# A decoder block on one core: where the later feed-forward's weights are loaded beside the expert slots

## The chip, the cores and the metric

One core of one Trainium2 chip runs the whole program. The metric is the device time of one execution in microseconds. The kernel before was run three times: 704.51 us is the median, with 700.71 and 704.6 as the others.

## The reference, cut to what matters

The input is 16 sequences of 128 tokens with 256 channels, in fp32. Six residual blocks follow each other. Each normalizes x and adds its result to x:

```
x = x + attention_0(layernorm(x))           # 16 heads
x = x + long convolution with the context, gated by layernorm(x)
x = x + mixture of experts(layernorm(x))    # a shared expert, and 1 of 8 experts for each token
x = x + attention_1(layernorm(x))
x = x + attention over the context tokens (masked)
x = x + feed-forward(layernorm(x))          # 256 -> 1024 -> 256, with ternary weights
```

Two of them matter here. In the mixture of experts, each token takes the expert with the largest router logit, and adds `gate * expert(x)` and `shared(x)`. Both are `silu(x @ wg) * (x @ wu) @ wd`. The last block's two weight matrices (256 x 1024 and 1024 x 256) are made ternary: the mean of the absolute weights sets a scale, the weights are scaled, rounded and clipped to -1, 0, 1. That preparation depends on no activation, so it can be done at any earlier point.

## The kernel before, in words

x stays in SBUF as 16 tiles of 128 tokens. Each engine has its own stream, in which the stages follow each other, and semaphores are the only order between engines. The change lies in `experts` (lines 954 to 1429), in its calls into `feed_forward` (`sync_weights`, `act_weights`, `pe_weights`, `dve_weights`, lines 1605 to 1663), and in `memory_attention`'s `mask` (line 1459).

The stage of the experts runs so:

- **Routing.** The 16 tiles are normalized and the router's logits made. The shared expert's gate and up projections (L1109, `pe_half`) run beside it and after it. Each token gets a row in a sorted array: expert by expert, padded to 23 slots of 128 rows.
- **Scatter.** POOL issues 16 indirect DMAs (L1292), which write the normalized rows to `sorted_x` in HBM. After all of them, SP loads the slots' rows (`load_slot`, L1192) into two buffers in turn. Slot t waits until slot t-2 has been transposed.
- **Shared downs.** The shared expert's down projection (`pe_shared`, L1162; four matmul instructions for each tile) is added to x by DVE (L1170 before the slots, L1394 behind them). `DOWN_FIRST` tiles, 8 here, are done ahead of the slots and the rest behind them. PE and DVE alternate over two PSUM banks, so PE's tile n waits for DVE's tile n-2.
- **Slots.** 23 slots with two steps in flight. PE transposes the rows (L1204), does gate and up (L1229, expert number from a register), transposes h (L1221) and does the down (L1239). ACT copies and does silu, DVE multiplies (L1265) and copies y (L1270), and POOL stores y to `sorted_y` (L1275).
- **Return.** When the last y is stored, POOL gathers the rows back tile by tile (L1304), DVE adds them with the gate (L1403), and the second attention begins.

Work for later stages is placed beside the slots, by `beside_slots`, once a step after the slot steps 2 to 5. Step index 0 and 1: ACT's sums of absolute values of the two weights (L1623), and on DVE two constants and the two passes over the mask (L1462, L1464). Index 2: PE's sum over partitions (L1636), which also waits until DVE has copied the fourth y, and DVE's chain of four small operations (L1650 to L1653). Index 3: the rounding of the first matrix on ACT (L1628) and DVE (L1658, L1663). The second matrix is rounded behind the slots ("later", "later end"), between the remaining downs of DVE.

The order on SP around it is: the first matrix in one DMA of 1 MB when half of the scatters are done, then (all scatters done) slots 0, 1 and 2, half of the second matrix, slot 3, the other half, the mask, and then slots 4 to 22. Behind that, when both matrices are rounded, SP loads 1.5 MB of bias and norm rows (L1603), and with `w_done` this waits for DVE's last pass L1663.

`slots` writes the first 6 steps out, runs the middle ones in a loop of two steps and writes the last ones out. PE has no loop there.

Of the kernel before, what the change touches and what calls it, by code (L numbers as in the profile page):

```python
# [9 lines left out]
NB = 16  # L10
# [9 lines left out]
NS = (NB * P - NE) // P + NE  # L20
# [18 lines left out]
def wait(eng, sem, value):  # L39

    if isinstance(value, int) and value <= 0:
        return
    eng.wait_ge(sem, value)
# [48 lines left out]
def build(nc, a, out, stages=6):  # L92

    ctx = ExitStack()
    with ctx:
# [3 lines left out]
        def sem(name):  # L99
            return ctx.enter_context(nc.semaphore(name))  # L100
# [69 lines left out]
        moe_y = sem("moe_y")  # L170
        w_o_loaded = sem("w_o_loaded")
        rows_loaded, route_loaded = sem("rows_loaded"), sem("route_loaded")
# [781 lines left out]
        def experts(conv_done, beside_slots):  # L954
# [15 lines left out]
            f = Front(0, NB, lambda eng, t: eng.wait_ge(s["x_conv"], t + 1), own_x=True)  # L970
# [128 lines left out]

            DOWN_FIRST = 8
            def pe_half(pe, n, p, kt):
                c, k = p // 2, p % 2
                if kt == 0:
                    pe.wait_ge([s["sh_silu"], s["sh_h"]][k], 2 * n + c + 1)
                    if p == 0:
                        pe.wait_ge(f.xnT, f.base_T + 4 * n + 4)
                mm = pe.matmul(ps[4 + p], w_sh_gu[:, kt, k * D + c * P:k * D + (c + 1) * P],  # L1109
                               xnT_all3[:, kt, ds(n * 512, 512)],  # L1110
                               start=(kt == 0), stop=(kt == KT - 1), skip_group_check=True)
                if kt == KT - 1:
                    mm.then_inc(s[f"sh_{'gu'[k]}{c}"], 1)
# [57 lines left out]
                                          ALU.add).then_inc(s["x_shared"], 1)  # L1171


            def slots(name, eng, body, ahead, behind):

                first, last = 6, (NS - ahead) - (NS - ahead) % 2
                for t in range(first):
                    body(eng, t, t % 2, t // 2)
                    if t >= 2:
                        beside_slots(name, eng, t - 2)  # L1180
                with eng.Fori(first // 2, last // 2) as i:
                    for u in range(2):
                        body(eng, 2 * i + u, u, i)
                for t in range(last, NS + behind):
                    body(eng, t, t % 2, t // 2)
                    beside_slots(name, eng, t)
# [3 lines left out]
            def load_slot(sp, t, u):  # L1190
                wait(sp, s["xsT_ps"], t - 1)
                sp.dma_start(xs[u], sorted_x[ds(t * P, P), :]).then_inc(s[f"xs{u}"], 16)  # L1192
# [116 lines left out]
            def sync(sp):  # L1309
                sp.wait_ge(conv_done, 2 + 2 * CH)  # L1310
                load_context(sp)
                sp.wait_ge(gathered[5], 16 * (NB // 2))
                beside_slots("sp", sp, "weights 0")
                sp.wait_ge(s["scattered"], 16 * (NB // 2))
                for t in range(3):
                    load_slot(sp, t, t % 2)
                beside_slots("sp", sp, "weights 1")
                load_slot(sp, 3, 1)
                beside_slots("sp", sp, "weights 2")
                sp.wait_ge(s["x_shared"], 2 + DOWN_FIRST)  # L1320
                beside_slots("sp", sp, "mask")
                with sp.Fori(2, 2 + NB // 2) as i:
                    for u in range(2):
                        load_slot(sp, 2 * i + u, u)
                for t in range(4 + NB, NS):
                    load_slot(sp, t, t % 2)

            def tensor(pe):
                pe.wait_ge(conv_done, 2 + 2 * CH - 2)
                keep_busy(pe, ps[3], ident, 9)  # L1330
                pe.wait_ge(conv_done, 2 + 2 * CH)
                pe.wait_ge(route_loaded, 48)
                pe.wait_ge(moe_loaded, 32)
                for t in range(NB + 3):
                    pe_route(pe, t, t % 2, t // 2)
                    if t < 5:
                        keep_busy(pe, ps[7], ident, 2)
                    if t >= 6:
                        q, kt = divmod(t - 6, 2)
                        pe_half(pe, q // 4, q % 4, kt)  # L1340
                pe_half(pe, 1, 2, 1)
                pe_positions(pe)
                pieces(pe, pe_piece)
                pe_shared(pe, 0, DOWN_FIRST)
                pe.wait_ge(s["expert"], 1)
                pe.wait_ge(moe_loaded, 64)
                experts = {0: load_expert(pe, 0)}
                pe.wait_ge(s["sh_h"], 10)
                pe.wait_ge(s["x_shared"], 2 + DOWN_FIRST)
                keep_busy(pe, ps[5], ident, 6)  # L1350
                pe_turn_slot(pe, 0, 0, 0)
                for t in range(NS + 1):
                    pe_slot(pe, t, t % 2, t // 2, experts)
                    if 2 <= t < 6:
                        beside_slots("pe", pe, t - 2)
                pe.wait_ge(s["silu"], NS)
                pe_shared(pe, DOWN_FIRST, NB)

# [12 lines left out]
            def vector(dve):  # L1371

                dve.wait_ge(route_loaded, 48)
                dve.tensor_copy(tri_bf, tri).then_inc(bf_ready, 1)
                dve.memset(ones_bf, 1.0).then_inc(bf_ready, 1)
                dve.memset(tick, 0.0).then_inc(s["sh_h"], 2)
                dve.engine_nop().then_inc(s["x_shared"], 2)
                routing(dve, dve_route, dve_piece)
                dve_positions(dve)
                pieces(dve, dve_piece)  # L1380
                dve_gate(dve)
                dve_shared(dve, 0, DOWN_FIRST)
                slots("dve", dve, dve_slot, 0, 1)
                for t in range(DOWN_FIRST, NB - 2):
                    dve_down(dve, t)
                    if t == 9:
                        beside_slots("dve", dve, "later")
                    if t == 11:
                        beside_slots("dve", dve, "later end")
                dve_gathered(dve, 0, 1)  # L1390

# [170 lines left out]
        def feed_forward(x_ready, before):  # L1562
# [4 lines left out]
            f = Front(0, 3 * NB, x_ready)  # L1567
# [9 lines left out]
            w32_3 = [kt_x(w32[0], INNER), kt_x(w32[1], D)]  # L1577
# [27 lines left out]
            def sync_weights(sp, part):  # L1605


                cp = lambda ap: ap.rearrange("(c p) n -> p c n", p=P)
                if part == "weights 0":
                    sp.dma_start(w32_3[0], cp(a["ffn_w1"])).then_inc(route_loaded, 16)  # L1610
                else:
                    k = INNER // P // 2
                    part = slice(0, k) if part == "weights 1" else slice(k, 2 * k)
                    sp.dma_start(w32_3[1][:, part, :], cp(a["ffn_w2"])[:, part, :]).then_inc(s["w_loaded"], 16)

            def act_weights(act, t):
                if t in (0, 1):
                    if t == 0:
                        act.wait_ge(route_loaded, 48 + 16)
                    else:  # L1620
                        act.wait_ge(s["w_loaded"], 32)
                    wait(act, s["w_abs"], t)
                    act.activation(junk_w, w32[t], ACT.Abs, accum_out=wabs[:, t:t + 1]  # L1623
                                   ).then_inc(s["w_abs"], 1)
                if t in (3, "later"):
                    act.wait_ge(s["w_chain"], 2)
                    k = 0 if t == 3 else 1
                    act.activation(w32[k], w32[k], ACT.Identity, bias=c_magic,  # L1628
                                   scale=wscale[:, k:k + 1]).then_inc(s["w_scaled"], 1)

            def pe_weights(pe, t):
                if t == 2:
                    pe.wait_ge(s["ones"], 1)
                    pe.wait_ge(s["w_abs"], 2)
                    pe.wait_ge(moe_y, 4)
                    pe.matmul(ps[7][:, D:D + 2], ones, wabs, start=True, stop=True).then_inc(s["w_tot"], 1)  # L1636

            def dve_weights(dve, t):
# [462 lines left out]
        def for_later_stages(name, eng, t):  # L2101

            if name == "sp":
                if t == "mask":
                    memory.sync(eng)
                else:
                    ffn.sync_weights(eng, t)
            if name in ("act", "pe", "dve"):
                ffn.weights[("act", "pe", "dve").index(name)](eng, t)
            if name == "dve":  # L2110
                memory.mask(eng, t)

        moe = experts(conv.summed, for_later_stages)

# [12 lines left out]
        memory = memory_attention(attn1.x_ready)  # L2127
# [105 lines left out]
```

## Time and profile before

| | |
|---|---|
| median of 3 runs | 704.51 us (700.71, 704.51, 704.6) |
| span of the profiled execution | 711.1 us |
| PE / DVE / ACT / POOL busy | 617.1 / 518.5 / 399.1 / 335.0 us |
| from the scatter's first issue to the first slot's transpose | 274.2 to 306.4 us |
| the slots, from the first transpose to the last y | 306.4 to 385.2 us |
| the rounded weights' last pass on DVE | 388.6 to 389.8 us |
| first work of the second attention on PE | 394.9 us |

The page gives no time of the profiled execution beside its span. That span is 6.6 us longer than the median of the runs and 10.4 us longer than the fastest of them. "Idle before" in brackets is the time for which an engine had nothing to run, with the instruction or transfer that ended it. A PE row's duration includes the modelled end of its last matmul.

### The profile page before, as it was taken

The page shows a single profiled execution, that of the slowest core. Times are in us where ns is not written, and L with a number is a line of the kernel's source. Part 1 is how long each engine was busy: PE and PEld are TensorE (multiplying, and loading weights), DVE is VectorE, ACT ScalarE, POOL GpSimd, SP SyncE. Part 2 cuts the span into 40 slices and gives each one's busy share as a digit, 9 for nine tenths or more (in the row PEclk, how much of TensorE's full clock was granted, in tenths as well). Part 3 has the DMA queues.
Part 4 walks back from the last instruction along what each step waited for, and adds up shares of the span by engine and source line. Part 5 has one row for each costly group of instructions (what it writes and reads, how often), then busy time and mean ns, then how long its engine had stood idle before and what let it go on. Part 6 is the DMA issues. An engine that isn't in the chain of part 4 may idle for free.

```text
span 711.1 us, 15833 instructions
## 1 busy us (share of the span) xinstructions
PE 617.1 (87%) x4620; PEld 471.5 (66%) x4622; DVE 518.5 (73%) x1187; ACT 399.1 (56%) x826; POOL 335.0 (47%) x650
## 2 busy tenths in 40 slices
PE   6999999989998899689999689999999677557776
PEld 5788888875555764477887567888887433245554
DVE  3688999985999674125224569999999578688994
ACT  2577777773333133034332246777777467778992
POOL 1234655444997344411112445333332568475882
PEclk9899999999999799799999779999999899859999
DMA  8301400011348701432221310000000000000101
GB/s 290 129 3 36 168 0 0 0 32 29 67 67 347 260 0 53 141 127 75 78 86 43 142 38 24 2 3 0 0 0 1 1 1 1 0 0 1 35 25 60
DMA packets 23043, 42.07 MB, mean 59 GB/s; under 512 B 3056, under 2 KB 18048, under 8 KB 21840
## 3 DMA queue, kind: packets, MB, share of 16 engines
q1 hardware_dynamic: 19504, 31.14, 13.9%
q0 software_dynamic: 3488, 10.28, 4.3%
q8 instruction: 29, 0.48, 0.3%
q14 instruction: 22, 0.18, 0.1%
HBM read 31.15 MB, written 10.26 MB: 58 GB/s over the span
## 4 chain that ended last, share of the span: by engine, by line
PE 55%; issue 14%; DVE 14%; POOL 8%; ACT 7%; DVEq 1%; DMA 1%; another core or an unknown queue 0%; SPq 0%; POOLq 0%; ACTq 0%
PE ps L1229 6%; PE ps L335 5%; PE ps L363 5%; PE ps L373 4%; PE ps L1109 4%; PE ps L383 3%; PE ps L322 3%; POOL ctx_sb L891 3%; PE ps L345 3%; DVE work L577 3%; PE ps L1239 3%; PE ps L802 2%; PE ps L1162 2%; DVE work L583 2%; PE ps L1883 2%
## 5 line engine op out<-in xcount | busy, mean ns | idle before, releaser
L498 ACT COPY wide<-ps 128x512 f32<-128x512 f32 x126 | 74.5, 593 | 43.3 <-PE ps L335 41.3
L230 POOL TENSOR_TENSOR var_eps<-mv,powers 128x1 f32<-128x1 f32 x80 | 16.8, 210 | 160.6 <-DVE mv L221 160.5
L577 DVE TENSOR_REDUCE work<-ps 128x8 f32<-128x1024 f32 x64 | 77.9, 1217 | 15.4 <-PE ps L322 12.1
L335 PE MATMUL ps<-ident,work 128*128 128x128 f32 x512 | 76.2, 281 | 3.9 <-ACT wide L498 1.8
L493 ACT ACTIVATE work<-work 128x1024 f32<-128x1024 f32 x64 | 68.4, 1069 | 20.0 <-DVE work L583 19.5
L583 DVE TENSOR_TENSOR work<-ps,work 128x1024 f32<-128x1024 f32 x64 | 77.8, 1216 | 0.6
L335 PEld LDWEIGHTS ps<-ident,work 128*128 128x128 f32 x512 | 59.2, 144 | 20.5 <-issue 14.3
L363 PE MATMUL ps<-xnT,w_qkv 128*128 128x128 f32 x256 | 41.0, 309 | 10.8 <-DVE work L583 9.3
L1275 POOL DMA_DIRECT2D sorted_y<-work x23 | 13.6, 591 | 78.0 <-DVE work L1270 78.0
L233 POOL TENSOR_TENSOR rstd<-var_eps,powers 128x1 f32<-128x1 f32 x80 | 45.1, 564 | 6.3
L1883 PE MATMUL ps<-w_o,wide 128*128 128x128 f32 x256 | 34.7, 294 | 15.0 <-DVE w_o L1929 15.0
L363 PEld LDWEIGHTS ps<-xnT,w_qkv 128*128 128x128 f32 x256 | 35.1, 212 | 17.2 <-issue 8.7
L1265 DVE TENSOR_TENSOR work<-work,ps 128x256 f32<-128x256 f32 x23 | 9.7, 421 | 49.5 <-ACT work L1259 49.5
L1229 PE MATMUL ps<-wide,work 128*128 x184 | 44.0, 382 | 0.0
L216 DVE BATCH_NORM_STATS2 bn<-x 128x6 f32<-128x256 f32 (+1 forms) x96 | 40.4, 421 | 4.7 <-DMA x<-in_x 2.5
L1883 PEld LDWEIGHTS ps<-w_o,wide 128*128 128x128 f32 x256 | 33.1, 209 | 15.6 <-issue 15.4
L936 DVE TENSOR_REDUCE wide<-ctx_sb 128x1024 f32 x32 | 39.0, 1220 | 5.5 <-POOL ctx_sb L891 1.2
L383 PE MATMUL ps<-w_qkv,xnT 128*128 128x256 f32 x128 | 39.0, 431 | 0.0
L322 PE MATMUL ps<-wide,work 32*128 32x256 f32 x512 | 36.7, 400 | 1.5 <-ACT work L510 0.8
L373 PE MATMUL ps<-xnT,w_qkv 128*128 128x128 f32 x256 | 37.9, 297 | 0.0
L1229 PEld LDWEIGHTS ps<-wide,work 128*128 128x128 f32 x184 | 33.1, 190 | 3.6
L373 PEld LDWEIGHTS ps<-xnT,w_qkv 128*128 128x128 f32 x256 | 35.3, 213 | 0.0
(226 smaller groups left out, 1572.9 us busy)
## 6 DMA issues: line engine op xcount, KB each, us to landing
wide<-in_expert_gu SPq DMA_DIRECT2D x1, 4096.0 KB, 15.3
sorted_x<-small POOLq DMA_DIRECT2D x1, 2944.0 KB, 11.7
work<-sorted_x SPq DMA_DIRECT2D x23, 128.0 KB, 2.0
sorted_y<-work POOLq DMA_DIRECT2D x23, 128.0 KB, 2.0
xn_all<-in_ctx_rev_t SPq DMA_DIRECT2D x1, 2048.0 KB, 10.6
small<-hank SPq DMA_DIRECT2D x16, 128.0 KB, 3.8
w_qkv<-hank SPq DMA_DIRECT2D x16, 128.0 KB, 3.8
wide<-in_expert_d SPq DMA_DIRECT2D x1, 2048.0 KB, 9.9
```

What stands on the lines that cost most here:

```text
L233: pool.tensor_tensor(f.rstd_v[u], f.var_eps[u], powers[:, 0:1], ALU.pow).then_inc(f.rstd, 1)
L322: mm = pe.matmul(S[i][:, c * 2 * P:(c + 1) * 2 * P], qT[u][rows, c, :], kTm[u][rows, c, :], start=True, stop=True, skip_group_check=True)
L335: mm = pe.transpose(turned(t, r)[:, h * P:(h + 1) * P], prob[r][:, h * P:(h + 1) * P], ident)
L363: mm = pe.matmul(Q[:, j * P:(j + 1) * P], w[:, c, j * P:(j + 1) * P], xT(c), start=(c == 0), stop=(c == KT - 1), skip_group_check=True)
L373: mm = pe.matmul(K[:, j * P:(j + 1) * P], w[:, c, D + j * P:D + (j + 1) * P], xT(c), start=(c == 0), stop=(c == KT - 1), skip_group_check= ...
L383: mm = pe.matmul(V[:, 0:D], xT(c), w[:, c, 2 * D:3 * D], start=(c == 0), stop=(c == KT - 1), skip_group_check=True)
L493: act.activation(prob2[g], prob2[g], ACT.Exp, scale=ATT_SCALE).then_inc(s["exp"], 1)
L498: act.copy(probT[r], turned(t, r)).then_inc(s["pT"], 1)
L577: dve.tensor_reduce(mxs[:, 8 * g:8 * g + 8], S2[g], AX.X, ALU.max).then_inc(s["mx"], 1)
L583: dve.tensor_tensor(prob2[g].rearrange("p (h k) -> p h k", k=P), S2[g], m.unsqueeze(2).broadcast_to([P, 2 * GH, P]), ALU.subtract).then_in ...
L1229: mm = pe.matmul(ps[2 * k + u][:, 0:NI], xsT[u][:, c * P:(c + 1) * P], w_ex_gu[:, c, ds(expert * (2 * NI) + k * NI, NI)], start=(c == 0), ...
L1883: pe.matmul(TB2[1 - u][:, c * P:(c + 1) * P], y[:, c * P:(c + 1) * P], diag[1 - u], start=(c % 4 == 0), stop=False, skip_group_check=True)
```

## The change

`DOWN_FIRST` becomes 12. The 1 MB load ahead of the slots is gone. The first matrix is loaded in two parts of 0.5 MB, and all four parts stand each behind the load of one slot's rows, slots 2 to 5. The work of later stages beside the slots starts after step 4 in place of 2 (`BESIDE_FROM`), the mask's two passes after steps 8 and 9, and 10 steps are written out ahead of the loop in place of 6. PE's sum waits for the sixth y in place of the fourth. Behind the slots, "later" stands behind DVE's down of tile 12 and "later end" behind tile 13.

```diff
-            DOWN_FIRST = 8
+            DOWN_FIRST = 12
...
+            BESIDE_FROM = 4
+
             def slots(name, eng, body, ahead, behind):
 
-                first, last = 6, (NS - ahead) - (NS - ahead) % 2
+                first, last = BESIDE_FROM + 6, (NS - ahead) - (NS - ahead) % 2
                 for t in range(first):
                     body(eng, t, t % 2, t // 2)
-                    if t >= 2:
-                        beside_slots(name, eng, t - 2)
+                    if t >= BESIDE_FROM:
+                        beside_slots(name, eng, t - BESIDE_FROM)
...
                 sp.wait_ge(gathered[5], 16 * (NB // 2))
-                beside_slots("sp", sp, "weights 0")
                 sp.wait_ge(s["scattered"], 16 * (NB // 2))
-                for t in range(3):
+                for t in range(6):
                     load_slot(sp, t, t % 2)
-                beside_slots("sp", sp, "weights 1")
-                load_slot(sp, 3, 1)
-                beside_slots("sp", sp, "weights 2")
+                    if t >= 2:
+                        beside_slots("sp", sp, f"weights {t - 2}")
                 sp.wait_ge(s["x_shared"], 2 + DOWN_FIRST)
                 beside_slots("sp", sp, "mask")
-                with sp.Fori(2, 2 + NB // 2) as i:
+                with sp.Fori(3, 2 + NB // 2) as i:
...
-                    if 2 <= t < 6:
-                        beside_slots("pe", pe, t - 2)
+                    if BESIDE_FROM <= t < BESIDE_FROM + 6:
+                        beside_slots("pe", pe, t - BESIDE_FROM)
...
-                    if t == 9:
+                    if t == 12:
                         beside_slots("dve", dve, "later")
-                    if t == 11:
+                    if t == 13:
                         beside_slots("dve", dve, "later end")
...
-                if part == "weights 0":
-                    sp.dma_start(w32_3[0], cp(a["ffn_w1"])).then_inc(route_loaded, 16)
+                if part in ("weights 0", "weights 1"):
+                    part = slice(0, 1) if part == "weights 0" else slice(1, 2)
+                    sp.dma_start(w32_3[0][:, part, :], cp(a["ffn_w1"])[:, part, :]).then_inc(route_loaded, 16)
                 else:
                     k = INNER // P // 2
-                    part = slice(0, k) if part == "weights 1" else slice(k, 2 * k)
+                    part = slice(0, k) if part == "weights 2" else slice(k, 2 * k)
...
-                        act.wait_ge(route_loaded, 48 + 16)
+                        act.wait_ge(route_loaded, 48 + 32)
...
-                    pe.wait_ge(moe_y, 4)
+                    pe.wait_ge(moe_y, 6)
...
-                memory.mask(eng, t)
+                memory.mask(eng, t - 4 if isinstance(t, int) else t)
```

## Rows read from the trace of the kernel before

**Rows 1.** The page: its first line, and its line of the engines' busy time.

```profile
span 711.1 us, 15833 instructions
PE 617.1 (87%) x4620; PEld 471.5 (66%) x4622; DVE 518.5 (73%) x1187; ACT 399.1 (56%) x826; POOL 335.0 (47%) x650
```

**Rows 2.** Windows: each engine's busy us (instructions), PE's granted clock, DMA share, GB/s.

```profile
288.40:294.10 5.70, 1.10 (x4) 0.68 (x5) 0.76 (x2) 0.00 (x0) 4.48 (x5) 0.93 0.68 264
294.10:304.40 10.30, 8.65 (x20) 6.21 (x20) 2.01 (x5) 0.00 (x0) 0.27 (x1) 0.54 0.12 38
395.00:402.00 7.00, 6.34 (x30) 5.80 (x31) 3.03 (x10) 1.00 (x3) 2.90 (x6) 0.55 0.28 106
```

**Rows 3.** Timeline (start, duration) of PE and DVE in the first shared downs.

```profile
288.89 1.10 PE L1162 MATMUL ps<-w_sh,work 128*128 128x256 f32 x4 [0.56 <-DVE x L1170]
293.56 0.42 DVE L1170 TENSOR_TENSOR x<-x,ps 128x256 f32 x1 [4.82 <-remote]
294.13 2.04 PE L1162 MATMUL ps<-w_sh,work 128*128 128x256 f32 x4 [4.14 <-issue]
297.09 0.75 DVE L1170 TENSOR_TENSOR x<-x,ps 128x256 f32 x2 [3.10 <-PE ps L1162]
304.97 1.58 PE L71 MATMUL ps<-ident 128*128 128x128 f32 x12 [0.71 <-DVE x L1170]
306.38 0.38 PE L1204 MATMUL ps<-ident,work 128*128 128x128 f32 x2
```

**Rows 4.** The chain of waits, behind the slots: start, duration, what.

```profile
384.70 1.74 PE ps L1162 x8
```

**Rows 5.** Timeline of POOL's last scatter and SP's first slot loads; page: issues to landing.

```profile
293.41 0.96 POOL L1292 DMA_INDIRECT sorted_x<-xn_all,small  x1 [0.30 <-issue]
295.82 0.82 SPq L1192 DMA_DIRECT2D work<-sorted_x  x2
work<-sorted_x SPq DMA_DIRECT2D x23, 128.0 KB, 2.0
```

**Rows 6.** Timeline of DVE and PE from the last y to the second attention.

```profile
384.74 0.42 DVE L1270 COPY work<-ps 128x256 f32<-128x256 f32 x1 [1.77 <-PE ps L1239]
385.60 0.42 DVE L1394 TENSOR_TENSOR x<-x,ps 128x256 f32<-128x256 f32 x1 [0.44 <-PE ps L1162]
388.60 1.22 DVE L1663 TENSOR_SCALAR xnT_all<-xn_all 128x2048 bf16<-128x2048 f32 x1
388.50 3.76 PE L1162 MATMUL ps<-w_sh,work 128*128 128x256 f32 x16 [0.34 <-DVE x L1394]
392.72 0.51 DVE L1403 SCALAR_TENSOR_TENSOR x<-wide,small,x 128x256 f32<-128x256 f32 x1 [1.79 <-DMA wide<-sorted_y,small]
394.85 1.68 PE L71 MATMUL ps<-ident 128*128 128x128 f32 x10 [2.59 <-issue]
396.99 0.49 DVE L1403 SCALAR_TENSOR_TENSOR x<-wide,small,x 128x256 f32<-128x256 f32 x1 [1.53 <-DMA wide<-sorted_y,small]
```

**Rows 7.** Timeline of POOL's first two gathers and of SP's rows.

```profile
388.30 1.64 POOL L1304 DMA_INDIRECT wide<-sorted_y,small  x1 [2.30 <-DMA sorted_y<-work]
390.24 0.97 POOL L1304 DMA_INDIRECT wide<-sorted_y,small  x1 [0.30 <-issue]
389.85 0.33 SPq L1603 DMA_DIRECT2D xn_all<-in_ffn_rows  x1
```

**Rows 8.** DMA queues in 390.4 to 390.9, 392.5 to 394.5 and 288 to 290.

```profile
q0 software_dynamic: 17, 0.07, 110.9%
...
q1 hardware_dynamic: 63, 0.77, 98.7%
...
q1 hardware_dynamic: 188, 0.77, 100.2%
```

**Rows 9.** Timeline of DVE and PE in the slots, beside the passes.

```profile
320.18 2.28 DVE L1464 TENSOR_REDUCE mem_cols<-work 128x16 f32<-128x2048 uint8 x1
323.54 0.35 PE L1636 MATMUL ps<-small 128*128 128x2 f32 x2 [0.61 <-DVE work L1270]
```

## The prediction, made before the change was run

> **What bounds the kernel now.** I read the page first. PE is busy for 87% of the 711.1 us span [rows 1], so the question of every edit is whether it moves PE's start or end in a stage. The chain of waits and the timeline then show two places near the change where PE is not the cause.
>
> The first is ahead of the slots. PE's third shared down starts at 288.89 and its fourth at 294.13. DVE's second add stands idle for 4.82 us before it runs at 293.56, and its third for 3.10 us [rows 3]. Meanwhile PE's granted clock falls to 0.54 for 294.1 to 304.4, that is mostly the 1.2 GHz level [rows 2]. So eight downs end at about 304.4 and the first slot is transposed at 306.38 [rows 3]. The rows of slot 0 are not what is late: SP issues them at 295.82, and a load of this kind lands after 2.0 us, so at 297.8 [rows 5].
>
> The second is behind the slots. The last y is copied at 384.74. POOL can gather at 388.30 [rows 7], DVE has idled 1.79 us when the first gathered tile arrives at 392.72, and PE starts the second attention at 394.85 after 2.59 us of idling [rows 6]. The end of the slots sets this path through y's store and the gather. The eight downs there run in its shadow.
>
> **Is the stall at 288 a cost of timed runs?** It delays the first slot by 306.38 - 297.9 = 8.5 us. The profiled execution is 6.6 us longer than the median run and 10.4 us longer than the fastest. If every timed run had the stall too, the median would have to find its 6.6 us somewhere else. I take it that timed runs lack most of it. This is my main choice. The case against it is a rival.
>
> **Ahead of the slots: four more downs.** They cost PE 1.74 / 2 = 0.87 us each at the full clock [rows 4]. The third down starts at 288.89 [rows 3]. Without the stall, six more (before) end at 288.89 + 5.2 = 294.1, ten more (after) at 288.89 + 8.7 = 297.6. From there DVE's add with its hand-overs takes about 0.7 us (0.42 for the add [rows 6], some 0.3 around it), and PE's twelve filler matmuls 306.38 - 304.97 = 1.4 us [rows 3]. Before: PE is ready at 296.2 and waits for the rows until 297.9. After: it is ready at 299.7. So the slots start 1.8 us later, **+1.8**. The bounds: +0.5 if the rows come only at 299 in timed runs, +3 at 0.94 us a down, which is what sixteen instructions behind the slots take with their pauses [rows 6] (10 x 0.07 more, and the last add).
>
> **Behind the slots: four downs fewer.** PE is relieved of 3.5 us. Since DVE already waits for the gather and PE for DVE, this is worth **0**. The cover is the path from the last y to the first gathered tile, 392.72 - 385.16 = 7.6 us. Four downs and two weight passes need 3.5 us of PE and 4 x 0.42 + 2 x 1.22 = 4.1 us of DVE, and fit. PE idles some 3.5 us longer there. The clock is at 0.55 just behind it already [rows 2], so I add nothing, and keep -1.5 to +1.5 for the stretch at the lower level beginning and ending elsewhere.
>
> **Behind the slots: the rows of 1.5 MB.** SP issues them when DVE's last weight pass has ended, at 388.60 + 1.22 = 389.82, seen at 389.85 [rows 6, 7]. After the change that pass stands behind two downs in place of four. DVE adds tile 12 at 385.60 to 386.0, rounds until 387.2, adds tile 13 until 387.5 and ends the last pass at 388.7. So SP's issue comes 1.15 us earlier against the slots' end. That matters because of the queues. At 390.4 to 390.9 only the gather's queue (q0) moves packets, so the first gather got in just ahead of the rows, which SP had issued 0.6 us or more before. In 392.5 to 394.5 the rows' queue (q1) is at 98.7% and q0 has no line at all [rows 8]: the second gather, issued at 390.24, is used at 396.99 in place of some 394, because it stands behind the rows [rows 6, 7]. With the rows 1.15 us earlier, they are ahead of the first gather too. Then the whole of it comes 1.15 us earlier than for the second gather, and the first has one tile less ahead of it (some 0.5 us): 396.99 - 1.15 - 0.5 = 395.3 in place of 392.7, **+2.6** where the order before was that of the trace. The bounds: 0, if the first gather still gets in first, and 396.99 - 392.72 = 4.3, the second gather's lateness.
>
> The Trainium skill (DMA: Bandwidth & Descriptors, Queues, rings and completion order) has each DMA engine take turns between the queues that have work, one packet at a time. By that rule the first gather would share the engines and come about 1 us late rather than 2.6, and the total would be 1.6 us less. The row of 392.5 to 394.5 does not agree: one queue had all of it.
>
> Timed runs before can already be on either side of this race, since the rows followed the gather by about half a microsecond here [rows 8]. Their two levels, 700.7 and 704.5, are 3.8 apart, which is of the race's size. So against the median I count **0** for it, and against the fastest run or the trace +2.6.
>
> **The loads moved.** The 1 MB load kept q1 at 100.2% in 288 to 290, and no scatter packet moved [rows 8]. POOL goes on issuing regardless, its last scatter at 293.41, and SP's loads follow at 295.82 [rows 5]: the scatter is bound by POOL's sixteen issues. Worth 0. Beside slots 0 to 3, SP now issues 2 MB of parts in place of 1 MB, and each row load stands behind one part at most. A part of 0.5 MB takes 1.4 us at the 0.77 MB in 2 us of [rows 8]. A row load is issued about two steps ahead of its use (23 slots in 78.4 us are 3.4 us a step, 6.8 for two) and lands in 2.0 [rows 5]: 3.4 < 6.8, so 0. The last part is issued after the transpose of slot 3, some 7 us after the first one, and has landed by 11; ACT's first sum comes after step 4, at about 14. The four DMA issues on SP are 0.4 us each on an engine that waits. The first y's stores can be held up behind the parts by the same effect as above. They have until the third y, two steps, so 0, with a rival below.
>
> **The passes moved.** The same instructions run two steps later. PE's sum waits for the y copied in its own step, as before, 0.61 us [rows 9]. The mask's reduction of 2.28 us now stands alone in a step of 3.4 us, in which DVE has 0.84 us of its own. Both 0, within 0.3. Ten written-out steps in place of six run the same instructions: 0, within 0.3.
>
> **Sum.** Against the trace: 711.1 - 8.5 + 1.8 + 2.6 = 707.0. Against the median: 704.5 + 1.8 + 0 = 706.3. I take **706.5 us**, slightly slower, within what a measurement can tell from no change. For this kernel that is about 1%, or 7 us.
>
> **The rivals.**
>
> A, the forecast, 0.50: 706.5, by its bounds from 703 to 710.
>
> B, the stall is real in timed runs and is the 1 MB load's doing, 0.24. It begins just where q1 fills [rows 3, 8], and the change takes that load away. Then the slots start at 299.7 in place of 306.4, -6.7, plus 0 to 2.6 for the rows: 698 to 700.5, about 700. Against it: the runs are shorter than the trace by the stall's size. In a third of this case (0.08 of the 0.24) it comes out below 697.5, with the clock at 2.4 GHz throughout the first slots and the gather ahead.
>
> C, the timed runs before lose clock ahead of the slots, 0.15. PE stands idle from 296.2 to 297.9 without the stall, and twelve downs fill that. A stretch of 7 to 10 us at 1.2 GHz costs 3.5 to 5 us, less the 1.8: 701.5 to 703.
>
> D, slower by over 1%, 0.06. The stores of the first y's are kept off the engines by parts, mask and row loads until the third y needs its buffer, and the slots stall there. The first y is stored about 8 us after the first transpose, and its buffer is needed two steps, 6.8 us, later. If q1 keeps q0 out for more than about 5 us from then, each further microsecond is paid in full. The four parts, the mask and six row loads are 3 MB, 8 us at the pace of [rows 8], which is for it; most of it goes before the first store, which is against. With 3 to 4 us there, 1.8 at the start and 2.6 at the gather: 712 to 713.
>
> E, the change does not act at all, since both places hide it: 704.5, 0.05.
>
> **How the numbers follow.** Faster by over 1% (below 697.5): 0.08. Slower by over 1% (above 711.5): 0.06, from D. Within: 0.86. The range from 699 to 710 holds A, C, E and the larger part of B, about 0.85.
>
> **What would show it.** Right: DVE has no idle of several microseconds in the twelve adds, the first transpose comes near 299.7, the slots last 78.4 us as before (306.38 to 384.74), SP's rows come 3.6 us behind the last y's copy in place of 4.7, and the first gathered add comes 10 us behind it in place of 8. Wrong: a stall among the downs again (the load had no part in it), the first gathered add at 8 us, a row load or a store that an engine in the slots waits for, or timed runs below 700 (then B, or C).

## The result, and the profile after

The changed kernel takes 707.19 us (median of 20 runs, 703.29 to 716.08), the kernel before in the same rounds 702.61 us (20 runs, 696.38 to 709.57). The ratio is 1.0073, with an interval of 1.0051 to 1.0094: slower by 0.7%, or 5.1 us. The ratio is of fast runs alone, which leaves out the slowest ones, 716.08 among them. The time lies inside the forecast's range of 699 to 710, and the change has the forecast's direction. Against the new median of before, the forecast's own step of +1.8 would have given 704.4, so the size was under half of what came. That 706.5 lies so near to 707.19 is luck: its base, the median of three runs, was 1.9 us too high, and its step 3.3 us too small.

The page of the changed kernel, its first line and its busy line, answers to [rows 1]:

```profile
span 702.9 us, 15806 instructions
PE 603.6 (86%) x4622; PEld 460.1 (65%) x4622; DVE 519.1 (74%) x1187; ACT 398.4 (57%) x826; POOL 327.4 (47%) x650
```

The profiled execution is 8.2 us *shorter* than the one of before, though the kernel is slower. The run that left this profile took 704.61 us, so a run is its span and 1.7 us. The profile of before was then of an execution of about 712.8 us, longer than each of its 20 timed runs. The windows of both kernels ahead of the change's place show where most of that came from (columns: length, busy us and instructions of PE, PEld, DVE, ACT and POOL, granted clock, DMA share, GB/s). Before:

```profile
0.00:60.00 60.00, 52.91 (x468) 44.22 (x472) 40.05 (x85) 32.45 (x64) 16.24 (x35) 0.94 0.36 125
240.00:274.00 34.00, 33.66 (x184) 23.07 (x183) 21.89 (x92) 10.08 (x21) 9.81 (x24) 0.87 0.19 74
```

After:

```profile
0.00:60.00 60.00, 52.16 (x498) 43.94 (x498) 43.10 (x89) 34.52 (x70) 16.77 (x35) 0.97 0.37 127
240.00:274.00 34.00, 33.66 (x173) 19.89 (x172) 20.36 (x80) 11.44 (x21) 13.93 (x26) 1.00 0.14 54
```

The granted clock was lower in two stages that the change does not touch, and the first scatter is issued at 274.2 before and 266.7 after: 7.5 us. A further 4.6 us lie behind PE's start of the second attention (394.85 to the end of the span is 316.2 us before, 391.26 to the end 311.6 after). DVE's timeline, with the eighth to tenth gathered adds before and then after, and the window of the first 7 us after PE's start in the changed kernel, which answers to the last line of [rows 2]:

```profile
424.56 1.27 DVE L1403 SCALAR_TENSOR_TENSOR x<-wide,small,x 128x256 f32<-128x256 f32 x3
416.50 1.27 DVE L1403 SCALAR_TENSOR_TENSOR x<-wide,small,x 128x256 f32<-128x256 f32 x3
391.26:398.26 7.00, 5.79 (x32) 4.96 (x32) 3.87 (x12) 1.37 (x4) 4.22 (x7) 0.77 0.16 42
```

From PE's start to the eighth add it is 29.7 us before and 25.2 after, with a granted clock of 0.55 and 0.77 at its beginning. The two places make more than 8.2 us because the change's own 4.0 (1.3 and 2.7, below) go the other way. So two spans say nothing of this change. Each place has to be measured from an event of its own stage: the first scatter for the start of the slots, the end of the last y's copy for what follows.

**The downs ahead of the slots.** DVE's and PE's timelines of the changed kernel, with POOL's last scatter and SP's first slot loads. They answer to [rows 3, 5].

```profile
285.80 0.96 POOL L1294 DMA_INDIRECT sorted_x<-xn_all,small  x1 [0.30 <-issue]
288.27 12.64 SPq L1194 DMA_DIRECT2D work<-sorted_x  x3
288.67 0.42 DVE L1170 TENSOR_TENSOR x<-x,ps 128x256 f32 x1 [5.17 <-remote]
289.24 8.81 PE L1162 MATMUL ps<-w_sh,work 128*128 128x256 f32 x32 [4.49 <-issue]
298.76 1.58 PE L71 MATMUL ps<-ident 128*128 128x128 f32 x12 [0.71 <-DVE x L1170]
300.18 0.38 PE L1206 MATMUL ps<-ident,work 128*128 128x128 f32 x2
```

The 1 MB load is gone, and the stall is still there: DVE idle for 5.17 us, PE for 4.49. Eight more downs then run without a pause, and the first transpose stands 33.5 us behind the first scatter (266.7 to 300.18), where it stood 32.1 us behind it before (274.24 to 306.38).

**Behind the slots.** DVE's, PE's, POOL's and SP's timelines from the last y. They answer to [rows 6, 7].

```profile
378.49 0.42 DVE L1272 COPY work<-ps 128x256 f32<-128x256 f32 x1 [1.77 <-PE ps L1241]
381.16 1.22 DVE L1664 TENSOR_SCALAR xnT_all<-xn_all 128x2048 bf16<-128x2048 f32 x1
382.04 1.20 POOL L1306 DMA_INDIRECT wide<-sorted_y,small  x1 [2.29 <-DMA sorted_y<-work]
382.40 0.33 SPq L1603 DMA_DIRECT2D xn_all<-in_ffn_rows  x1
389.15 0.48 DVE L1403 SCALAR_TENSOR_TENSOR x<-wide,small,x 128x256 f32<-128x256 f32 x1 [6.78 <-DMA wide<-sorted_y,small]
391.26 2.47 PE L71 MATMUL ps<-ident 128*128 128x128 f32 x10 [8.77 <-issue]
391.77 0.48 DVE L1403 SCALAR_TENSOR_TENSOR x<-wide,small,x 128x256 f32<-128x256 f32 x1
```

The last y's copy ends at 378.91. SP issues the rows 3.5 us behind it (4.7 before), the first gathered add comes 10.2 us behind it (7.6 before), and PE's start 12.4 us (9.7 before): +2.7. SP issues the rows 0.36 us behind POOL's first gather (382.40 and 382.04), and 1.55 us behind it before (389.85 and 388.30, [rows 7]). The order of the two issues is the same, but the rows' packets now come first. The DMA queues of 383.2 to 386.8 hold one line. It answers to the second of [rows 8]:

```profile
q1 hardware_dynamic: 95, 1.17, 97.3%
```

The slots in between take 78.3 us (300.18 to 378.49), as before (78.4).

### The profile page after: what moved, and what is told of

It is laid out like the page before. It is cut to its first block, busy times and chain, and to the rows that moved or that the text cites. A ratio compares the mean times of both kernels' runs of the same rounds, so it can differ in the third digit from the quotient of the medians.

```text
span 702.9 us, 15806 instructions
## 1 busy us (share of the span) xinstructions
PE 603.6 (86%) x4622; PEld 460.1 (65%) x4622; DVE 519.1 (74%) x1187; ACT 398.4 (57%) x826; POOL 327.4 (47%) x650
## 4 chain that ended last, share of the span: by engine, by line
PE 58%; issue 15%; DVE 13%; ACT 7%; POOL 4%; DMA 1%; DVEq 1%; SPq 0%; ACTq 0%; POOLq 0%
PE ps L802 6%; PE ps L1231 6%; PE ps L335 5%; PE ps L363 4%; PE ps L1109 4%; PE ps L373 3%; PE ps L322 3%; PE ps L383 3%; PE ps L345 3%; PE ps L1241 2%; PE ps L1884 2%; DVE work L577 2%; DVE work L583 2%; PE ps L400 2%; PE ps L1162 2%
## 5 line engine op out<-in xcount | busy, mean ns | idle before, releaser
L363 PE MATMUL ps<-xnT,w_qkv 128*128 128x128 f32 x256 | 37.9, 293 | 10.1 <-DVE work L583 8.2
L363 PEld LDWEIGHTS ps<-xnT,w_qkv 128*128 128x128 f32 x256 | 32.3, 198 | 16.4 <-issue 7.4
L383 PE MATMUL ps<-w_qkv,xnT 128*128 128x256 f32 x128 | 37.0, 413 | 0.0
L373 PE MATMUL ps<-xnT,w_qkv 128*128 128x128 f32 x256 | 35.5, 284 | 0.0
L345 PE MATMUL ps<-wide,work 128*32 128x128 f32 x1024 | 34.6, 276 | 0.7 <-DVE wide L627 0.6
## 6 DMA issues: line engine op xcount, KB each, us to landing
sorted_x<-small POOLq DMA_DIRECT2D x1, 2944.0 KB, 11.8
xn_all<-in_ctx_rev_t SPq DMA_DIRECT2D x1, 2048.0 KB, 10.5
```

Of the source, the lines that this page charges most:

```text
L345: mm = pe.matmul(O[VW * k:VW * k + VW, r * P:(r + 1) * P], va[u][:, GH * r + k, :], probT[r][:, k * P:(k + 1) * P], start=True, stop=True, ...
L363: mm = pe.matmul(Q[:, j * P:(j + 1) * P], w[:, c, j * P:(j + 1) * P], xT(c), start=(c == 0), stop=(c == KT - 1), skip_group_check=True)
L373: mm = pe.matmul(K[:, j * P:(j + 1) * P], w[:, c, D + j * P:D + (j + 1) * P], xT(c), start=(c == 0), stop=(c == KT - 1), skip_group_check= ...
L383: mm = pe.matmul(V[:, 0:D], xT(c), w[:, c, 2 * D:3 * D], start=(c == 0), stop=(c == KT - 1), skip_group_check=True)
```

## Experiments

Each experiment was run beside the kernel before, on the same chip, and each ratio is against it. Two figures are read from each trace: the first transpose behind the first scatter, called the *start*, and the first gathered add behind the end of the last y's copy, called the *gather*. For before and after they are 32.1 and 7.6, 33.5 and 10.2. Each trace is one execution.

### e1: the moved loads and passes alone

```diff
-            DOWN_FIRST = 12
+            DOWN_FIRST = 8
...
-                    if t == 12:
+                    if t == 9:
                         beside_slots("dve", dve, "later")
-                    if t == 13:
+                    if t == 11:
```

> The changed kernel with eight downs ahead of the slots again, and the second matrix's two DVE passes again behind the downs of tiles 9 and 11. What is left of the change is where the four weight parts and the beside-work stand. Theory (the twelve downs carry all of the change): ratio to the kernel before 1.000, between 0.997 and 1.003; rows issued 4.7 us behind the last y's copy, first gathered add about 8 us behind it. Rival (the moved loads or passes cost something): 1.004 to 1.007, with a wait in the slots that shows it. Rival (the 1 MB load made the stall among the downs): 0.990 to 0.993, and no idle of DVE over 2 us among the downs.

Ratio 0.9989 (0.9956 to 1.0021), start 29.4, gather 7.4, and the rows are issued 4.7 us behind the last y's copy. The moved loads and passes cost nothing that can be measured. An add of DVE's timeline of e1:

```profile
292.31 0.42 DVE L1170 TENSOR_TENSOR x<-x,ps 128x256 f32 x1 [3.78 <-remote]
```

The stall is there without the 1 MB load, as it is in the changed kernel. The rival by which the load made it (B) falls.

### e2: the twelve downs alone

```diff
-            DOWN_FIRST = 8
+            DOWN_FIRST = 12
...
-                    if t == 9:
+                    if t == 12:
                         beside_slots("dve", dve, "later")
-                    if t == 11:
+                    if t == 13:
```

> The kernel before with nothing changed but twelve downs ahead of the slots, and the two passes behind the downs of tiles 12 and 13. Theory: all of the cost, ratio 1.006 to 1.008, the first gathered add about 10 us behind the last y's copy. Rival (cost comes from the moved loads): 1.000 to 1.002.

Ratio 1.0104 (1.0055 to 1.0153), start 34.5, gather 10.4. All of the loss is in this edit. The middle lies above the expectation, and its interval holds the changed kernel's 1.0073. DVE's first gathered add in e2, with the same idle time before it as in the changed kernel (6.78):

```profile
393.40 0.48 DVE L1403 SCALAR_TENSOR_TENSOR x<-wide,small,x 128x256 f32<-128x256 f32 x1 [6.92 <-DMA wide<-sorted_y,small]
```

### e3: the rows behind the first gathered tile

The edit is in the changed kernel, on SP, ahead of the rows' load:

```diff
+                sp.wait_ge(gathered[0], 16)
```

> The changed kernel, but SP issues the 1.5 MB of rows only when the first gathered tile has landed. Theory (2.6 us of the loss are the first gather standing behind the rows): the first gathered add comes 7 to 8 us behind the last y's copy in place of 10.2, and the ratio to the kernel before falls from 1.0073 to 1.0035 (1.001 to 1.005). Rival (the gather's lateness is hidden, or is given back by PE's clock in the second attention): 1.006 to 1.008 with the gather early all the same.

Ratio 1.0015 (0.9977 to 1.0053), start 35.4. The timeline of e3, with the last y's copy, SP's issue of the rows and the first gathered add:

```profile
380.73 0.42 DVE L1272 COPY work<-ps 128x256 f32<-128x256 f32 x1 [1.77 <-PE ps L1241]
387.31 0.33 SPq L1604 DMA_DIRECT2D xn_all<-in_ffn_rows  x1
387.32 0.48 DVE L1404 SCALAR_TENSOR_TENSOR x<-wide,small,x 128x256 f32<-128x256 f32 x1 [2.70 <-DMA wide<-sorted_y,small]
```

The gather comes at 6.2 us in place of 10.2, sooner than the 7 to 8 expected and than in the kernel before. The interval excludes the rival's 1.006 to 1.008: the gather's lateness is neither hidden nor given back. The eighth gathered add shows that too. It comes 37.6, 40.1, 39.0 and 40.8 us behind the last y's copy in the four traces with a late gather (after, e2, e7, e9), and 35.3, 35.9, 33.0, 36.0, 35.6 and 35.4 in e1, e3, e4, e5, e8 and e10, with an early one. (e6, in between at 9.3, has 38.8.) The trace of before has 39.4 with an early gather, through its lower clock there.

### e4: the same wait in the kernel before

SP issues the rows behind four gathered tiles:

```diff
+                sp.wait_ge(gathered[2], 32)
```

> The kernel before, but SP issues the rows only when the first four gathered tiles have landed. If timed runs of the kernel before often have the first gather behind the rows, as the spread of its runs made me think: 0.996 to 0.998. If the order in its trace is the usual one, only the second tile is earlier, and it has slack: 0.998 to 1.001. The second gathered add comes 3 us or more earlier against the last y's copy in either case.

Ratio 0.9974 (0.9941 to 1.0006), start 30.9, gather 6.7. DVE's first two gathered adds in e4:

```profile
387.26 0.48 DVE L1404 SCALAR_TENSOR_TENSOR x<-wide,small,x 128x256 f32<-128x256 f32 x1 [0.90 <-DMA wide<-sorted_y,small]
390.40 0.48 DVE L1404 SCALAR_TENSOR_TENSOR x<-wide,small,x 128x256 f32<-128x256 f32 x1
```

The second comes 9.8 us behind the last y's copy, where it came 11.8 behind it before: 2.0 us earlier, not the 3 or more expected. The interval reaches both expectations. It doesn't quite exclude a race that the runs before lose as a rule either: 10.4 - 6.7 = 3.7 us would be a ratio of 0.9947. That is settled by e7.

e3 and e4 are of the same rounds, both keep the rows behind the gather, and they differ by twelve and eight downs (and by the moved loads of e1): 1.0015 against 0.9974, or 2.9 us. It is the one pair of times that shows the cost at the start apart from the gather, and the two intervals overlap.

### e7: the rows early, and nothing else

```diff
-                    if t == 9:
+                    if t == 8:
                         beside_slots("dve", dve, "later")
-                    if t == 11:
+                    if t == 9:
                         beside_slots("dve", dve, "later end")
```

> The kernel before with one edit: DVE's two passes over the second matrix stand behind the downs of tiles 8 and 9 in place of 9 and 11, so SP issues the rows about 1 us earlier, with eight downs ahead as before. Theory: this alone puts the first gather behind the rows, first gathered add about 10.3 us behind the last y's copy in place of 7.5, ratio 1.002 to 1.005. Rival (the gather's lateness in the changed kernel comes from something else): 7.5 us, ratio 1.000.

Ratio 1.0051 (1.0021 to 1.0082), start 31.3. The timeline of e7, with the last y's copy, SP's issue and the first gathered add:

```profile
378.11 0.42 DVE L1270 COPY work<-ps 128x256 f32<-128x256 f32 x1 [1.77 <-PE ps L1239]
382.03 0.33 SPq L1603 DMA_DIRECT2D xn_all<-in_ffn_rows  x1
388.95 0.48 DVE L1403 SCALAR_TENSOR_TENSOR x<-wide,small,x 128x256 f32<-128x256 f32 x1 [4.05 <-DMA wide<-sorted_y,small]
```

The gather comes at 10.4 us with eight downs ahead. Two DVE passes of 1.2 us, moved ahead of one and of two downs, cost 0.5% of the kernel, because they let 1.5 MB into the DMA queues 1.2 us sooner. POOL issues the first gather 0.36 us ahead of the rows here:

```profile
381.67 1.20 POOL L1304 DMA_INDIRECT wide<-sorted_y,small  x1 [2.30 <-DMA sorted_y<-work]
```

If the runs of before lost this race as a rule, e7 would have cost nothing. Its interval lies wholly above 1.

### e5: half of the scatters

```diff
-                for t in range(NB):
+                for t in range(NB // 2):
                     pool.indirect_dma_start(out=sorted_x, ...
...
-                sp.wait_ge(s["scattered"], 16 * (NB // 2))
```

> The kernel before with POOL issuing eight of the sixteen scatters; the rows of tiles 8 to 15 stay zero in the sorted array, and SP loads the slots' rows behind the eight. In every trace so far PE's sums of the shared downs reach DVE 3 to 5 us late while the later scatters are being issued, and come on time when they have ended. Theory (the stall belongs to the scatters): with the last scatter ended before the first down, no gap over 1.5 us among the downs, and the first transpose 5 to 8 us earlier after the first scatter (about 24 in place of 31). Rival (the stall belongs to PE, DVE or their order): a gap of 3 us or more at the third or fourth down as before.

One run, 693.98 us beside 702.95 for the kernel before. POOL's last scatter, then DVE's and PE's timelines of e5:

```profile
277.87 0.96 POOL L1292 DMA_INDIRECT sorted_x<-xn_all,small  x1 [0.30 <-issue]
282.92 0.75 DVE L1170 TENSOR_TENSOR x<-x,ps 128x256 f32 x2 [0.43 <-issue]
284.74 0.42 DVE L1170 TENSOR_TENSOR x<-x,ps 128x256 f32 x1 [1.06 <-PE ps L1162]
289.23 0.42 DVE L1170 TENSOR_TENSOR x<-x,ps 128x256 f32 x1 [0.44 <-PE ps L1162]
283.49 5.60 PE L1162 MATMUL ps<-w_sh,work 128*128 128x256 f32 x24 [0.56 <-DVE x L1170]
291.21 0.38 PE L1204 MATMUL ps<-ident,work 128*128 128x128 f32 x2
```

No idle over 1.1 us is left among the adds, and the start is at 22.4 (the first scatter is issued at 268.8). In this run the packets of the last scatters have also gone by 280, ahead of the first down at 281.0. So the stall belongs to scatters that are issued or still moving while the downs run; e5 can't tell POOL's issuing from the packets.

### e9: the changed kernel with half of the scatters

The edit is that of e5, in the changed kernel.

> The changed kernel with POOL issuing eight of the sixteen scatters (the rows of tiles 8 to 15 stay zero in the sorted array). Without the stall each further down costs its PE time alone: first transpose 22.37 + 4 x 0.87 = 25.9 us after the first scatter, against 22.37 for eight downs, with no gap over 1 us. If it is 24 or less, the downs ahead are partly hidden even here. The first gathered add comes 10.2 us behind the last y's copy.

PE's timeline of e9, with ten downs without a pause and the first transpose:

```profile
281.58 9.23 PE L1162 MATMUL ps<-w_sh,work 128*128 128x256 f32 x40 [0.56 <-DVE x L1170]
292.94 0.38 PE L1206 MATMUL ps<-ident,work 128*128 128x128 f32 x2
```

One run took 701.43 us. Start 26.0, gather 10.5. Four more downs cost 26.0 - 22.4 = 3.6 us where no scatter disturbs and the slots' rows are there early: their PE time and no less.

### e10: twelve of the scatters

```diff
-                for t in range(NB):
+                for t in range(12):
                     pool.indirect_dma_start(out=sorted_x, ...
...
-                sp.wait_ge(s["scattered"], 16 * (NB // 2))
+                sp.wait_ge(s["scattered"], 16 * 4)
```

> The kernel before with twelve of the sixteen scatters issued (tiles 12 to 15 left out). In the traces the late signals begin about when the twelfth scatter is issued. If they come with a scatter being issued while the downs run, the first downs here meet the ninth or later scatters and a gap shows; if they come with the number of scatters in flight beyond eleven or so, none or under 1 us. First transpose 22.5 to 24 us after the first scatter without a gap, 27 or more with one.

One run, 702.6 us beside 704.68 for the kernel before. DVE's, PE's and SP's timelines of e10:

```profile
291.51 0.75 DVE L1170 TENSOR_TENSOR x<-x,ps 128x256 f32 x2 [2.68 <-PE ps L1162]
292.07 6.24 PE L1162 MATMUL ps<-w_sh,work 128*128 128x256 f32 x20 [2.00 <-DVE x L1170]
292.35 0.82 SPq L1192 DMA_DIRECT2D work<-sorted_x  x2
300.44 0.38 PE L1204 MATMUL ps<-ident,work 128*128 128x128 f32 x2
```

A shorter gap of 2.0 us on PE, and a start of 26.1, between the expectations. Here the last two scatters were issued beside the downs, so a few such scatters already bring a stall. How many it takes stays open. DVE's late add at 291.51 runs 2.1 us after POOL's last issue has ended (289.4), while packets of the scatters still move. A second thing shows: the last scatter was issued by 289.4, yet SP could load only at 292.35, 2.9 us later, where the lag is 1.5 us with sixteen ([rows 5]: 294.37 to 295.82). The DMA queues of e10, first two lines in 287 to 289, last line in 290 to 292.3:

```profile
q1 hardware_dynamic: 120, 0.49, 88.6%
q0 software_dynamic: 3, 0.01, 1.3%
...
q0 software_dynamic: 144, 0.39, 43.7%
```

The 1 MB load, issued at 285.81, kept the scatters' queue nearly empty until it was through. With sixteen scatters POOL's issuing covers that.

### e6: four downs ahead, and the rows behind the gathers

```diff
-            DOWN_FIRST = 8
+            DOWN_FIRST = 4
...
+                sp.wait_ge(gathered[2], 32)
...
-            mask32 = work[:, 3072:3584].bitcast(I32)
+            mask32 = xnT.bitcast(I32)
```

> The other direction: four downs ahead of the slots in place of eight, twelve behind, and the rows issued behind the first four gathered tiles; the mask is loaded into another buffer, as its old one is still in use. Theory: each down ahead costs 0.87 us of PE, so the first transpose comes 3.5 us earlier after the first scatter than with eight (about 27.3); behind the slots the twelve downs now outlast the gather, and the first gathered add comes 8.5 to 9 us behind the last y in place of 6.7. Net 1 to 2 us faster than the rows' wait alone (0.9974): 0.994 to 0.997. Rival (the downs behind cost as much as they save): 0.997 to 1.000.

Ratio 0.9963 (0.9932 to 0.9994), start 26.2, gather 9.3. Both figures went the expected way and a little further: 4.6 us less at the start than in e4 (3.5 expected), and 2.6 more at the gather (9.3, with 8.5 to 9 expected). The ratio cannot be told from e4's, and its interval reaches the rival's 0.997 to 1.000 too. PE's timeline of e6 shows what bounds the start now:

```profile
287.44 1.10 PE L1162 MATMUL ps<-w_sh,work 128*128 128x256 f32 x4 [2.06 <-issue]
293.40 2.90 PE L71 MATMUL ps<-ident 128*128 128x128 f32 x12 [4.86 <-DVE x L1170]
```

The fourth down is done by 288.5, and the fillers start at 293.40: the last add waits out the stall.

### e8: eight banks, so that the stall costs PE nothing

```diff
+            def down_ps(t):
+                return ps[t if t < 8 else t % 4][:, 0:D]
...
-                        pe.wait_ge(s["sh_h"], 2 * n + 4)
-                        pe.wait_ge(s["x_shared"], 4 * n + j + 1)
+                        pe.wait_ge(s["sh_h"], 2 * n + 4 if n < 1 else 10)
+                        wait(pe, s["x_shared"], 4 * n + j - 1 if 4 * n + j >= 8 else 0)
                         for c in range(KT):
-                            mm = pe.matmul(ps[j % 2][:, 0:D], ...
+                            mm = pe.matmul(down_ps(4 * n + j), ...
...
+                sp.wait_ge(gathered[2], 32)
```

> The kernel before with the rows issued behind the first four gathered tiles, and with the eight downs ahead of the slots in eight PSUM banks in place of two, so that PE waits for no add of DVE until the last. Theory (PE works on during the stall and only its signals to DVE come late): PE's eight downs run in 7 us without a gap, its clock stays at 2.4 GHz, and the first transpose comes when the last late signal is in, about 25 to 26.5 us after the first scatter in place of 31; ratio 0.989 to 0.993, against 0.9974 for the rows' wait alone. Rival (PE itself stands still while the scatters are issued): a gap remains, 30 us, and 0.996 to 0.999.

DVE's loop over the first adds is written out as well. Ratio 0.9888 (0.9837 to 0.9940), the fastest kernel of this study that does all of the work. PE's timeline of e8, then DVE's:

```profile
282.54 7.07 PE L1166 MATMUL ps<-w_sh,work 128*128 128x256 f32 x32
294.98 2.90 PE L71 MATMUL ps<-ident 128*128 128x128 f32 x12 [5.37 <-DVE x L1397]
...
287.43 0.42 DVE L1397 TENSOR_TENSOR x<-x,ps 128x256 f32<-128x256 f32 x1 [3.16 <-issue]
291.66 0.42 DVE L1397 TENSOR_TENSOR x<-x,ps 128x256 f32<-128x256 f32 x1 [3.81 <-remote]
293.09 1.74 DVE L1397 TENSOR_TENSOR x<-x,ps 128x256 f32<-128x256 f32 x5 [1.01 <-remote]
```

PE runs all eight downs in 7.07 us with no gap. They are done by 289.6, and DVE then still has six of the eight results to add; it stands still until 291.66. At the end five adds run back to back. So PE works on through the stall, and DVE gets to its results late. Whether PE's signals arrive late or DVE takes them up late, the trace does not tell. The start is at 27.3 (first scatter 270.34, first transpose 297.67), 0.8 us above the upper end of the expectation: the fillers take 2.90 us in place of 1.58, at a granted clock of 0.50 (1.2 GHz) behind an idle of 5.37 us. Against e4 the ratio is 0.9% better, some 6 us, and the start 3.6 us earlier. The two were timed in different rounds, and their intervals leave that difference open.

## Why the prediction was right or wrong, step by step

**"I take it that timed runs lack most of it" (the stall).** Wrong, and it was called the main choice. All nine traces with sixteen scatters have the stall, with DVE idle for 2 to 5 us once or twice among the adds. The prediction compared a span with the times of runs. Since a run is its span and 1.7 us, the execution before was 8.3 us longer than the 704.5, not 6.6. In the other eleven traces the first scatter is issued at 269.5 on average (266.7 to 274.3), and the second attention's start on PE lies 312.7 us ahead of the end (309.2 to 315.7). The trace of before has 274.2 and 316.2: 4.8 us more ahead of the stage and 3.5 behind it, 8.3 together. The windows shown above have a lower PE clock in both places. The step took a difference of whole spans for the size of one stall because both were some 8 us. A window ahead of the stage could have cast doubt on it: 0.87 of the clock in 240 to 274. Of the prediction's signs of being wrong the first one came, a stall among the downs again. In its sum against the trace the 8.5 us taken off for the stall stand in for 8.3 us of other stages, so that its 707.0 is near for the wrong reason.

**"Ahead of the slots: four more downs", +1.8.** Mis-sized through that choice. It let the slot rows' arrival at 297.9 be the limit for eight downs and absorb half of the added PE time. With the stall, the downs end well behind the rows in both kernels, and all four are on the path. In the four traces with eight downs in two banks and sixteen scatters (32.1, 29.4, 30.9, 31.3: before, e1, e4, e7) the start averages 30.9, in the three with twelve (33.5, 34.5, 35.4: after, e2, e3) 34.5. That is +3.5, as 4 x 0.87 gives, and e9 against e5 gives +3.6 without the stall. Traces of one group differ by up to 2.7 us: after against before alone would give +1.3, within the stated bounds by chance. The upper bound of +3 was too low.

**"Behind the slots: four downs fewer", 0.** Right. In the changed kernel DVE idles 6.78 us ahead of the first gathered add, and PE 8.77 us. The -1.5 to +1.5 kept for the clock behind it is not resolved: single traces differ there by more, for reasons that no run here separates.

**"Behind the slots: the rows of 1.5 MB", +2.6.** Right in place, mechanism and size (+2.7 in the trace; rows at 3.5 us, 3.6 foretold). e7 makes it alone, e3 takes it away. **Setting it to 0 against the median** was wrong: by e7 the runs of before do not lose the race as a rule, and its 1.0051 (3.6 us) is what losing it costs. Whether some of them lose it stays open. Twenty runs of before spread from 696.4 to 709.6, so the 3.8 us between two of three runs could not carry the choice.

**The turn-taking between queues.** The Trainium skill (DMA: Bandwidth & Descriptors, Queues, rings and completion order) has each DMA engine alternate, packet by packet, between the queues that have work. The prediction's estimate by it was a term 1.6 us smaller. The row of the changed kernel, 97.3% for q1 and no line for q0 while the gather waited, disagrees again, and the measured term is the full one. Only from 387.0 to 388.0 do both queues move packets, and q1 still has 59 to 81% there.

**"The loads moved", "The passes moved", 0.** Right, by e1, and by slots that last 78.3 us.

**The rivals.** B falls by e1: the stall comes without the load too. C supposed idle time without a stall; it has no ground left. D did not occur: no engine in the slots waited for a row or a store. E supposed that the change does nothing, and the ratio's interval excludes it. A, the forecast, had the right range with half of its mechanism. The measured sum is 3.5 + 2.7 = 6.2 us. The ratio gives 5.1 (3.6 to 6.6), e2 alone 7.3 (3.9 to 10.7).

## What to carry to other kernels

Work that is put ahead of a start costs its full time unless the trace shows that engine idle there in every run, and a stall in the trace counts as present until a run without it is seen; compare spans stage by stage, from an event of the stage, since PE's clock moved whole spans by more than this change did. A large load that nobody waits for is not harmless: look at which small transfers are issued close to it, even shortly ahead of it (0.36 us here), and make it wait for those that someone needs (here one wait on SP). Where an engine hands small results to another one through two buffers, more buffers can cover results that are taken up late (e8).

## What the runs showed of the hardware that was not expected

- While indirect scatters are being issued or are still moving, DVE can get to PE's finished results 2 to 5 us late, though PE's matmuls go on (e8: 7.07 us for 32 without a gap, with DVE idle for 3.81 us in between). In e3 that lasts 1.1 us beyond the last scatter's landing (the add at 289.74, SP's first load at 288.63). With no scatter left beside the downs it is on time (e5, e9: no gap over 0.6 us on PE). It is not every signal: in e8 DVE's multiply L1139 at 282.93 runs after 2.54 us of idling for PE with scatters issued around it, as the one at 281.43 does in e5 without. Why the signals of the downs are late was not tried and stays open.
- A transfer of 1.5 MB on the hardware queue kept a software-queue gather of 128 KB out: 97.3% against no line for 3.6 us, and then both queues for 1 us. The gathered tile came at 10.2 to 10.5 us in place of 6.2 to 7.8. A 1 MB load did the same to the scatters (e10: 88.6% against 1.3%).
- The order of the two issues did not decide who came first. With the rows 1.55 us behind the gather (before), the gather's packets went first, from 390.6. With the rows 0.36 us behind it (after, e7), theirs did, in the changed kernel from 383.3. In e3, where neither was in the other's way, the gather's first packet moved 1.8 us after its issue (384.28 to 386.1) and the rows' 0.9 us after theirs (387.31 to 388.2). So 1.2 us in the time of one issue is 2.7 us on the path.
